# Softmax weights read from PSUM in the two edge stages of a graph network kernel

## The reference

```
edge_index = jnp.stack([src, dst])
x = x + gnn0(layernorm(x), edge_attr_8, Wq, Wk, Wv, Wo, src, dst)
x = x + ffn0(layernorm(x)[None], ...)[0]             # 8 experts, the best one
x = x + gnn1(layernorm(x), W, attn_src, attn_dst, edge_index, edge_type_8)
x = x + ffn1(layernorm(x)[None], ...)[0]             # 8 experts, the best two

# gnn0: 8 heads of 32 channels
attn = jnp.einsum('ehd,ehd->eh', k[src], q[dst]) + attn_bias
m = segment_max(attn, dst);  a = jnp.exp(attn - m[dst])
a = a / segment_sum(a, dst)[dst]
out = segment_sum(v[src] * a[:, :, None], dst).reshape(n, FEAT) @ Wo.T

# gnn1: values picked by the edge's relation
h_all = jnp.einsum('nf,rof->rno', x, W).reshape(r, n, h, d)
h_src = h_all[edge_type, src];  h_dst = h_all[edge_type, dst]
scores = leaky(sum(h_src * attn_src) + sum(h_dst * attn_dst))
w = jnp.exp(scores - amax[dst]);  w = w / segment_sum(w, dst)[dst]
out = segment_sum(h_src * w[..., None], dst)
```

## Time and profile before

| | |
|---|---|
| time, median of 3 runs (lowest to highest) | 4402.75 us (4402.75 to 4403.49) |
| the profiled execution's own time | 4394.72 us |
| its span, first to last instruction | 4392.9 us |
| mean granted clock of TensorE | 0.877 of full speed |
| busy over the span: TensorE, VectorE, GpSimd, ScalarE | 81%, 64%, 54%, 44% |
| attention over the edges | 178 to 1420 us |
| relational layer | 2621 to 3800 us |

### The profile page before, as it was taken

The page is one execution under the profiler, slowest core; times in us unless marked ns, Lnnn a source line. Parts: engine busy times, 40 slices in busy tenths (PEclk is TensorE's granted clock), DMA queues, the critical chain, the costliest instruction groups (busy, mean ns, idle before and its releaser), DMA issues. The chain is left out here.

```text
span 4392.9 us, 68229 instructions
## 1 busy us (share of the span) xinstructions
PE 3573.9 (81%) x18253; PEld 2801.0 (64%) x18254; DVE 2827.4 (64%) x7798; ACT 1936.9 (44%) x5274; POOL 2391.3 (54%) x2486
## 2 busy tenths in 40 slices
PE   7788888888887999699989986777777777585883
PEld 4466666666665899699954445555566665474772
DVE  5599999999998455211122227788888888732446
ACT  2455555555553333233323336555555555342220
POOL 5477777777774354200022227777777777355331
PEclk9899999999998999899989997787877787755996
DMA  6577777777774311111134446555555555322336
GB/s 202 191 203 205 203 205 206 205 206 206 205 204 131 133 40 37 52 36 36 35 124 180 174 184 185 162 160 160 169 164 160 160 171 163 120 91 84 106 108 211
DMA packets 264927, 656.46 MB, mean 149 GB/s; under 512 B 52764, under 2 KB 138936, under 8 KB 248872
## 3 DMA queue, kind: packets, MB, share of 16 engines
q0 software_dynamic: 129536, 396.58, 31.6%
q1 hardware_dynamic: 128024, 249.81, 16.4%
q10 hardware_dynamic: 7056, 6.43, 0.4%
HBM read 521.34 MB, written 131.29 MB: 149 GB/s over the span
## 5 line engine op out<-in xcount | busy, mean ns | idle before, releaser
L278 POOL DMA_INDIRECT attn_KV<-kv_tab,attn_stage x880 | 932.3, 1059 | 279.6 <-issue 251.1
L1841 POOL DMA_INDIRECT rel_V<-h_tab,rel_stage x880 | 886.9, 1008 | 309.0 <-issue 237.3
L1944 PE MATMUL rel_SP<-rel_V,rel_OH 128*128 128x264 f32 x1760 | 610.9, 487 | 2.4 <-DVE node L2011 1.6
L379 PE MATMUL attn_QP<-node,attn_OHT 128*128 x1760 | 504.3, 412 | 11.1 <-issue 5.7
L391 PE MATMUL attn_SP<-attn_KV 128*128 128x264 f32 x1760 | 491.5, 405 | 24.3 <-DVE node L493 23.9
L1944 PEld LDWEIGHTS rel_SP<-rel_V,rel_OH 128*128 128x128 f32 x1760 | 380.7, 237 | 76.3 <-ACT rel_OH L1879 8.1
L391 PEld LDWEIGHTS attn_SP<-attn_KV 128*128 128x128 f32 x1760 | 343.2, 200 | 97.2 <-issue 40.2
L2011 DVE TENSOR_TENSOR node<-node,rel_SP 128x264 f32 x880 | 366.3, 416 | 55.7 <-PE rel_SP L1944 35.3
L379 PEld LDWEIGHTS attn_QP<-node,attn_OHT 128*128 128x128 f32 x1760 | 331.3, 201 | 61.8 <-issue 15.8
L1737 PE MATMUL pr_H<-WX,pr_YT 128*128 128x512 f32 x784 | 345.8, 594 | 0.0
L454 DVE TENSOR_TENSOR attn_KV<-attn_KV,attn_QP 128x512 f32<-128x512 f32 x440 | 298.0, 677 | 57.6 <-DMA attn_KV<-kv_tab,attn_stage 57.4
(11 more groups left out here) (396 smaller groups left out, 6924.8 us busy)
## 6 DMA issues: line engine op xcount, KB each, us to landing
rel_OHT<-dst_rows SPq DMA_DIRECT2D x55, 1024.0 KB, 6.0
h_tab<-pr_H SPq DMA_DIRECT2D x49, 1056.0 KB, 4.0
attn_KV<-kv_tab,attn_stage POOLq DMA_INDIRECT x880, 3.8
rel_V<-h_tab,rel_stage POOLq DMA_INDIRECT x880
pair_Y<-y SPq DMA_DIRECT2D x105, 130.0 KB, 2.1
kv_tab<-qkv_KV SPq DMA_DIRECT2D x49, 256.0 KB, 2.3
mix_Y<-y_out SPq DMA_DIRECT2D x49, 256.0 KB, 4.3
attn_runs<-runs SPq DMA_DIRECT2D x55, 192.0 KB
```

The lines of the kernel that those rows point to most:

```text
L278: pool.indirect_dma_start(out=KV[:, i * IT + u, 0:2 * FEAT], out_offset=None, in_=d["kv_tab"][:, :], in_offset=bass.IndirectOffsetOnAxis(a ...
L379: mm = pe.matmul(QP[(2 * i + v) % BANKS][:, (u % 2) * FEAT:(u % 2 + 1) * FEAT], OHT[:, u, :], query(blks[v]), start=True, stop=True)
L1841: pool.indirect_dma_start(out=V[:, i * IT + u, :], out_offset=None, in_=d["h_tab"][:, :], in_offset=bass.IndirectOffsetOnAxis(ap=stage[:, ...
L1944: pe.matmul(SP[(c * IT + u) % SUMS][:, 0:NUMC], OH[:, j * IT + u, :], V[:, j * IT + u, :], start=True, stop=True).then_inc(s["sums"], 1)
```

## The change

In both edge stages the transposed weights W get a PSUM bank of their own, WB, and `weigh` reads its second input from there (`weights`, a view of W with step and head exchanged) in place of the last columns of the value rows in SBUF. ScalarE's copy of W into these columns stays, and so does VectorE's wait for it. The transpose into WB now waits until all eight weighings of the group before have read the bank. The bank comes from the query banks in attention (three to two) and from the sum banks in the relational layer (five to four). No instruction is added, removed or moved on any engine. The operands of these change: 440 weighings and 55 transposes in each stage, and ScalarE's 55 copies.

```diff
@@ attention_layer @@
-    BANKS = 3
+    BANKS = 2
...
-    assert BANKS == RING and PAIRS % BANKS == 2
+    assert PAIRS % BANKS == 0
...
-        T, W = CH[:, 0:P], CH[:, P:2 * P]
+        WB = ctx.enter_context(nc.psum_tensor("attn_WB", [P, 512], F32))
+        T, W = CH[:, 0:P], WB[:, 0:P]
+        weights = W.rearrange("p (h s) -> p s h", s=IT)
...
-                            mm = pe.matmul(QP[(2 * i + v) % BANKS][:, (u % 2) * FEAT:(u % 2 + 1) * FEAT], OHT[:, u, :], query(blks[v]),
+                            mm = pe.matmul(QP[v % BANKS][:, (u % 2) * FEAT:(u % 2 + 1) * FEAT], OHT[:, u, :], query(blks[v]),
...
                     if has(g, G):
                         pe.wait_ge(s["rows_f"], 3 * g + 3)
                         pe.wait_ge(s["exp"], g + 1)
+
+                        need(pe, s["weighted"], g * PAIRS)
                         pe.transpose(W, EX[:, :], m.ident[:, :]).then_inc(s["w_turned"], 1)
...
-                        dve.tensor_tensor(keys, keys, QP[(2 * i + v) % BANKS][:, :].rearrange("p (s c) -> p s c", c=FEAT),
+                        dve.tensor_tensor(keys, keys, QP[v % BANKS][:, :].rearrange("p (s c) -> p s c", c=FEAT),
...
-                        dve.tensor_tensor(rows, rows, KV[:, at:at + 2, 2 * FEAT:ROW].unsqueeze(3).to_broadcast([P, 2, HEADS, DH]),
+                        dve.tensor_tensor(rows, rows, weights[:, 2 * v:2 * v + 2, :].unsqueeze(3).to_broadcast([P, 2, HEADS, DH]),
                                           ALU.mult).then_inc(s["weighted"], 1)
@@ relational_layer @@
-    SUMS = 5
+    SUMS = 4
...
-        T, W = CH[:, 0:P], CH[:, P:2 * P]
+        WB = ctx.enter_context(nc.psum_tensor("rel_WB", [P, 512], F32))
+        T, W = CH[:, 0:P], WB[:, 0:P]
+        weights = W.rearrange("p (h s) -> p s h", s=IT)
...
+                        need(pe, s["weighted"], g * PAIRS)
                         pe.transpose(W, EX[:, :], m.ident[:, :]).then_inc(s["w_turned"], 1)
...
-                        dve.tensor_tensor(rows, rows, V[:, at:at + 2, FEAT:NUMC].unsqueeze(3).to_broadcast([P, 2, HEADS, DH]),
+                        dve.tensor_tensor(rows, rows, weights[:, 2 * v:2 * v + 2, :].unsqueeze(3).to_broadcast([P, 2, HEADS, DH]),
                                           ALU.mult).then_inc(s["weighted"], 1)
```

## The result

| | before | changed |
|---|---|---|
| median (lowest to highest) | 4402.75 us (4399.4 to 4403.49) | 4306.73 us (4301.71 to 4309.55) |
| ratio of the runs, 95% interval | | 0.9782 (0.9765 to 0.9799) |
| span of the profiled execution | 4392.9 us | 4307.2 us |
| attention stage, first to last instruction | 1229.2 us | 1184.1 us |
| relational stage | 1186.6 us | 1134.9 us |

The kernel is 96 us or 2.2% faster, where 87 us were forecast. The two edge stages are 45.1 and 51.7 us shorter in the profiles (before, attention ran from 177.1 to 1406.3 us and the relational stage from 2620.8 to 3807.4 us). The rest is 11 us longer, 8.4 of it in the expert phase near the end (266.4 to 274.8 us); this did not come again in a second profile (e4: 266.2 us), so it belongs to that execution.

What follows compares the result with a forecast made beforehand. Gather issue on GpSimd was taken to bound both edge stages, VectorE close behind in attention. Gains of 52 + 35 = 87 us from 4394.72 gave 4307.7; the median's extra 8.0 made it 4316, range 4302 to 4348.

Steps and rivals of the forecast that it cites:

- Relational stage, -52 forecast: Relational stage: 880 gathers fall from 1009 to 949 ns, gather issue still sets the pace; 52 us less.
- Attention, -35 forecast: Attention stage: VectorE's waits for gathered rows vanish and it becomes the bound; 35 us less.
- GpSimd's new wait: Attention: GpSimd should now wait for the sums that free its buffers, about 1.1 us a period.
- The weighing from PSUM: Both edge stages: the weighing takes as long with its second input from PSUM; cost 0, upper end 26 us.
- rival A: Weighings: reading PSUM makes each 60 ns longer, attention loses 26 of its 35 us, total 4342; chance 0.10.
- parts 4 to 6: Edge stages: fewer query banks, fewer sum banks and the transpose's new wait are covered by existing waits; cost 0 each.
- part 5: Relational stage: with four sum banks, VectorE's 33.3 us wait for sums, doubled, would be 0.65 us a period; cost 0.
- Rival D: Attention: two query banks make TensorE's clock fall and the kernel slower, up to 4489 us; chance 0.04.
- a sign of D: Attention: a granted TensorE clock under 0.9 would show the forecast wrong through a falling clock.

Runs made afterwards that it cites:

- e4: The changed kernel run again with no edit: 4295.6 us, ratio 0.9777 to the kernel before.
- e2: The change in the relational stage alone, attention as in the kernel before: 4343.6 us, ratio 0.9887.
- e1: The change in the attention stage alone, relational layer as in the kernel before: 4350.4 us, ratio 0.9899.
- e3: The changed kernel with its banks and new wait kept, but the weighings reading weights from SBUF: 4417.0 us, ratio 1.0051 to the kernel before.
- e11: The kernel before with two query banks and four sum banks, nothing else: 4785.1 us against 4779.8 on that chip, ratio 1.0012.
- e12: The changed kernel with one small factor operation a period moved from VectorE to ScalarE: 4850.7 us, ratio 1.0150 to the kernel before on that chip.
- e6: The changed kernel without the rescaling of the 256 value columns in both edge stages: 4817.7 us, kernel before 4751.1 on that chip.
- e9: The changed kernel without the value columns' rescaling, run once more on another chip: 4862.7 us, kernel before 4790.9 there.
- e5: The changed kernel with the relational stage's products reading a constant SBUF tensor instead of the PSUM query bank: 4806.5 us, kernel before 4751.1 on that chip.
- e8: The kernel before with each weighing replaced by an in-place multiplication by 1.0, one SBUF input: 4805.8 us, kernel before 4751.1 on that chip.

## Why the prediction was right

It held the time, 4306.73 us, in its range with a point of 4316, and by the mechanism it named.

1. Relational stage, -52 forecast, -51.7 measured, -51.1 in e2's median. The working (60 ns for each of 880 gathers, with VectorE's wait as the room for it) needs no change. Of that wait 1.16 us a period was left, where 1.0 was forecast.
2. Attention, -35 forecast, -45.1 measured, -44.3 in e1's median. The mechanism held (GpSimd's bound passed to VectorE), and the size of this term was off. VectorE's period, from one rescaling to the next, went from 21.85 to 21.01 us, 0.83 less. I had taken the listed waits for rows, 0.68 a period or 37 us over 55 periods, called them 36 and took 35. Part of what was missing is in how a wait is listed: the list counts from the end of the instruction before, but in both kernels a product that waits for nothing starts 0.08 us before that end. With this lost overlap added, 45 waits in the stretch of the earlier trace rows (an estimate: 45 x 0.08 = 3.6 us on top of 34.7) come to 0.75 us a period. The remaining 0.08 are in small part the faster weighings (8 x 4 ns); start to start, VectorE's additions and one small operation are shorter too. 0.83 x 54 is 45 us. GpSimd's new wait came to 31 us over the stage, 0.6 us a period, where 1.1 was forecast, since it was not held up at all in the first groups.
3. The weighing from PSUM: 0 forecast, -4 ns measured, so rival A is out. The Trainium skill, "VectorE: DVE Perf Modes", section "The TRN2 errata", would have it 65 ns longer (an estimate from its 120 and 58 cycles); 673 ns against 677 decide against that here.
4. Query banks, sum banks and the new wait (parts 4 to 6): 0 forecast, and in the changed kernel nothing of it reaches the pace, as VectorE's idle time in attention was 0.03 us a period. The new wait in the relational stage is there as forecast, 26.9 us for L1985 or 0.5 us a period, and covered. In part 5 the 33.3 us are 0.65 us a period as they stand, and doubled they would be 1.3; the wait fell to 26.5 us. But the reason I gave was not the whole of it. I looked for waits and found each covered. e3 shows that, while the gathers could still be held up, the new arrangement cost 22 us by longer gathers and not by a wait. Whether the banks or the weights' own bank and its wait do it stays open: e11 has the fewer banks alone, and on its chip they cost nothing that could be measured.
5. Rival D had TensorE's clock fall in attention through the two query banks. On the first chip it rose, from 0.96 to 1.00, and e3 with the same banks had 1.00 as well. On the chip of e12 it was 0.87, below the 0.9 that the prediction gave as a sign of D, but also 0.90 in e11 without the change in the weighing, and both have the pauses.

That VectorE sets attention's pace after the change rests on the profile (99.8% busy, no wait listed, GpSimd held to 21.0 us a group from the 16th on). No experiment took work from VectorE and gained; e6, e9 and e12 did not.

There is luck in it too: the prediction knew nothing of the pauses, and had its launches fallen on one of the other chips, the change would probably have made the kernel slower. The whole changed kernel was not run there, but its attention stage was, line for line, in e5: 1484.4 us, in a kernel that took 55 us more than the one before on that chip. If the kernel before spent 1972 to 1982 us outside the edge stages there and 1345 to 1350 us in the relational one, as e5 to e8 did, its attention took 1417 to 1432 us (an estimate, from one run), and the change made that stage 50 to 70 us longer. e12, the changed kernel but for one small operation, was 1.5% slower over four runs. e8 has short gathers and three query banks and lost as much as e5, so the banks are not needed for the loss. Whether GpSimd's faster issue makes the pauses more frequent, or both hang on a third thing, no run here tells; nor whether the chip or the time at which it was used made the difference, as each chip was seen at one time only.

## What to carry to other kernels

Look for the engine that is never held up rather than the one with the highest busy share: GpSimd at 78% busy was the bound, and the gap before each gather told it. Where gathers are issued from GpSimd, count VectorE's operations that read two SBUF tensors, or that read and write SBUF with one input as fast as e8's (0.41 us for 128x512), and give one input to PSUM where a bank can be had. And run a part that should be neutral by itself, and the whole on more than one chip: here the part was not neutral, and where the edge stages paused, the kernels with short gathers were 55 to 72 us slower, not 96 us faster.

## What the runs showed of the hardware

- A gather's issue is stretched by a VectorE operation with two SBUF inputs (1.37 to 1.42 us for 0.95) and by e8's single-input multiplication, which takes 0.41 us for 128x512 (1.40 us), not by one of the same size with an input in PSUM (0.95 us) nor by the 0.68 us sum over a single SBUF input (0.95 us). The VectorE operation can be the one that waits: 0.57 us for 0.41 in e8.
- A gather held by a weighing ended 0.82 to 0.84 us after the weighing did (352 of the 354 that began up to 0.5 us behind one, kernel before).
- When the operation starts matters. In the kernel before, a weighing that began 0.39 us into a gather cost most of all, 1.89 us; others that began within 0.01 us of that point left it at 0.95 us:

```profile
1004.55 1.89 POOL L278 DMA_INDIRECT attn_KV<-kv_tab,attn_stage  x1 [0.30 <-issue]
...
1004.94 0.68 DVE L471 TENSOR_TENSOR attn_KV<-attn_KV 128x512 f32<-128x512 f32 x1
```

- Chips differed by more than the change is worth: the kernel before took 4394.8 us on one and 4751 to 4791 on three others. In the profiles of e5 to e12 all of the added time lies in the two edge stages, whose periods are written out in the program one after the other.
